# Involution on one core: the kernel products of two units issued together, their accumulations behind both

## The chip, the core and the metric

The program runs on one core of a Trainium2 chip. The metric is device time in microseconds (us) of one execution, and the median over the runs is compared.

## The reference, cut to what matters

A pair representation z of 64 x 64 positions and 32 channels goes through two triangle multiplications, two triangle attentions and a transition (not touched here), and then through an involution of 5 x 5 taps whose kernel is computed from the pixel itself:

```
z = relu(gamma * (x @ w1 + b1 - mean) / sqrt(var + 1e-3) + beta)     # 32 -> 8 channels
kern = (z @ w2 + b2).reshape(B, H, W, 25, 8)                          # 25 taps x 8 groups
patches = 25 shifted images of the padded x                           # (.., 25, 4, 8)
out = einsum('bhwpg,bhwpng->bhwng', kern, patches)                    # sum over the taps
```

## The kernel before

An image lies as 128 partitions by 1024 columns: four blocks of 16 rows, each with 32 channels on its own 32 partitions. One PSUM bank holds 512 columns, so every tile is computed in two halves (`ch` 0 and 1).

The involution is cut into 25 units (`UNITS`). Units 0 to 4 ("B") treat the middle column of taps for all four blocks at once, with the whole 128 rows of TensorE. Units 5 to 24 ("A") are `i` = 0 to 4 times `g` = 0 to 3: unit 5 + 4i + g treats block g and, stacked on the four groups of 32 partitions, the four horizontal shifts of tap row i. Its kernel product contracts 32 partitions only, those of block g (row group g of TensorE). So two units next to each other always use different row groups.

A unit passes through these steps, each on its own engine with its own queue in program order:

- TensorE computes the kernel product, two matmuls (halves) into two banks of one of three kernel buffers, `kern_banks(u)` = buffer u % 3 (L1544 for B, L1546 for A), and raises `inv_kern` with the second.
- For a unit in `ON_DVE`, VectorE adds the bias and multiplies by the shifted image in one instruction, PSUM to a product buffer (L1102). For one in `ON_POOL` = (1, 5, 8, 10, 13, 16, 20, 22), ScalarE evicts the kernel to `gate` or `th` (L832) and GpSimd multiplies (L590).
- TensorE adds the products up in banks 0 and 1 by matmuls with the identity (`ident`, accumulations n = 0 to 3, one B unit each, L1524) or with a stacked identity (`stackid`, n = 4 to 8, four A units each in four column groups, L1526). An fp32 matmul shows as two MATMUL instructions in the profile. Accumulation (n, ch) waits for the products of its units.

TensorE's order is written out by hand: units in turn, and behind each what the table `ACC_AFTER` lists for it:

```
ACC_AFTER = {5: ((1, 0), (1, 1)), 6: ((2, 0),), 7: ((3, 0),), 9: ((0, 0),), 11: ((0, 1),), 14: ((2, 1), (4, 0)),
             17: ((3, 1), (4, 1)), 19: ((5, 0),), 20: ((5, 1),), 23: ((6, 0), (6, 1)), 24: ((7, 0), (7, 1), (8, 0), (8, 1))}
```

Before its kernel product, unit u waits until unit u - 3 has left the kernel buffer: until VectorE's product (`inv_prod_dve`) or ScalarE's eviction (`inv_kbuf`) of it. There are 16 product buffers; units 16 to 24 wait for the accumulation of the unit whose buffer they take (`inv_acc`). Units 3, 4 and 5 have an extra dummy matmul ahead of them (`keep_warm`, L1116). The images that the A units read are copied into place by DMAs from SyncE (L469). When the last accumulation is done, VectorE and ScalarE copy the two result halves and they are stored.

Of the kernel before, what the change touches and what calls it, by code (L numbers as in the profile page):

```python
# [25 lines left out]
C = 32  # L26
# [8 lines left out]
KS = 5  # L35
# [26 lines left out]
def build_program(nc, z_rows, z_cols, vecs, consts, selrow, tm_w, tm_rows, ta_w, ta_qk, pt_w, inv_w1, inv_w2, out):  # L62
    with ExitStack() as ctx:
        def sb(name, cols, dt=F32, parts=128):
            return ctx.enter_context(nc.sbuf_tensor(name, [parts, cols], dt))
# [10 lines left out]
        def shared(name):  # L76

            for norm in NORMS:
                if name in (norm + "_xn", norm + "_x"):
                    return "ln_" + name[len(norm) + 1:], 2 * [n for n in NORMS if n not in LN_BIAS_FOLDED].index(norm)  # L80
                if name.startswith(norm + "_"):
                    return "ln_" + name[len(norm) + 1:], 2 * NORMS.index(norm)
            if name == "tm1_gtanh":
                return name, 0
            if name[:4] == "tail" and name[5] == "_":
                return "tail" + name[5:], 3 * int(name[4])
            for kind in ("tm", "ta"):
                if name[:2] == kind and name[2] in "01" and name[3] == "_":
                    return kind + name[3:], int(name[2]) * RAISES.get(name[4:], 2)
            return name, 0  # L90

        def sig(name):

            name = shared(name)[0]
            if name not in signals:
                signals[name] = ctx.enter_context(nc.semaphore(name))
            return signals[name]
# [22 lines left out]
        def K(name):  # L120
            i = CONST.index(name)
            return cst[:, 128 * i:128 * i + 128]
# [14 lines left out]
        w2s = sb("w2s", 2 * KS * 128, F32R)  # L137
# [61 lines left out]
        zst = sb("zst", F, F32R)  # L199
# [10 lines left out]
        def half(buf, ch):  # L210
            return buf[:, ch * HALF:(ch + 1) * HALF]
# [92 lines left out]
        def cols_of(buf, m):  # L304
# [7 lines left out]
        UNITS = [("B", i, None) for i in range(KS)] + [("A", i, g) for i in range(KS) for g in range(GB)]  # L312
# [5 lines left out]
        ACC_AFTER = {5: ((1, 0), (1, 1)), 6: ((2, 0),), 7: ((3, 0),), 9: ((0, 0),), 11: ((0, 1),), 14: ((2, 1), (4, 0)),  # L318
                     17: ((3, 1), (4, 1)), 19: ((5, 0),), 20: ((5, 1),), 23: ((6, 0), (6, 1)), 24: ((7, 0), (7, 1), (8, 0), (8, 1))}
# [42 lines left out]
        def kern_banks(i):  # L362
            return psum[:, (2 + 2 * (i % 3)) * HALF:(4 + 2 * (i % 3)) * HALF]
# [7 lines left out]
        WARM_UNITS = (3, 4, 5)  # L371
# [737 lines left out]
        def _(pe):  # L1109
            mm = nc.tensor.matmul  # L1110

            def keep_warm(b, n, operand=cst):


                for _ in range(n):
                    mm(bank[b][:, 0:256], operand[:, 0:128], operand[:, 0:256], start=True, stop=True, skip_group_check=True)  # L1116
# [391 lines left out]
            def wait_product(u):  # L1508

                if u == 0:  # L1510
                    pe.wait_ge(sig("inv_sum"), 1)
                elif u in ON_POOL:
                    pe.wait_ge(sig("inv_prod_pool"), ON_POOL.index(u) + 1)
                else:
                    pe.wait_ge(sig("inv_prod_dve"), ON_DVE.index(u) + 1)

            def accumulate(n, ch):

                for u in ACCUMULATE[n]:
                    wait_product(u)  # L1520
                for u in ACCUMULATE[n]:
                    kind, i, g = UNITS[u]
                    if kind == "B":
                        last = mm(bank[ch], K("ident"), half(prod[u % NPROD], ch), start=n == 1, stop=False, skip_group_check=True)  # L1524
                    else:
                        last = mm(bank[ch][C * g:C * g + C, :], stackid[:, :], half(prod[u % NPROD], ch), start=False, stop=n == 8,  # L1526
                                  skip_group_check=True)
                if n == len(ACCUMULATE) - 1:
                    last.then_inc(sig("inv_done"), 1)
                elif ch == 1:  # L1530
                    last.then_inc(sig("inv_acc"), 1)

            for u, (kind, i, g) in enumerate(UNITS):
                if u in WARM_UNITS:
                    keep_warm(0, 1)
                if u >= 3:
                    if u - 3 in ON_POOL:
                        pe.wait_ge(sig("inv_kbuf"), ON_POOL.index(u - 3) + 1)
                    else:
                        pe.wait_ge(sig("inv_prod_dve"), ON_DVE.index(u - 3) + 1)  # L1540
                for ch in range(2):
                    pe.wait_ge(sig("inv_zst"), ch + 1)
                    if kind == "B":
                        last = mm(half(kern_banks(u), ch), w2s[:, (KS + i) * 128:(KS + i + 1) * 128], half(zst, ch), start=True, stop=True)  # L1544
                    else:
                        last = mm(half(kern_banks(u), ch), w2s[C * g:C * g + C, i * 128:(i + 1) * 128], half(zst, ch)[C * g:C * g + C, :],  # L1546
                                  start=True, stop=True)
                last.then_inc(sig("inv_kern"), 1)
                for n, ch in ACC_AFTER.get(u, ()):
                    accumulate(n, ch)  # L1550


# [104 lines left out]
```

## Time and profile before

| | us |
|---|---|
| median of 3 runs | 228.76 (228.7 to 229.5) |
| profiled execution | 229.4 |
| its span in the profile | 226.9 |
| TensorE busy | 207.0 |
| VectorE busy | 140.9 |
| ScalarE busy | 126.7 |
| GpSimd busy | 96.0 |

Times in the rows count from the start of the span. Busy time of an engine leaves out its waits and its register work. The ends of matmuls are modelled, and matmuls overlap, so the distance between two starts says more than the length of one. A row of the timeline merges instructions of one kind that follow each other and gives their number; the time in brackets is the idle time before them and the instruction that ended it.

### The profile page before, as it was taken

Reading aid. Unit: us, or ns where it says so; the run is one execution under the profiler, and the core shown is the slowest. Engines: PE = TensorE matmul, PEld = TensorE weight load, DVE = VectorE, ACT = ScalarE, POOL = GpSimd, SP = SyncE. Lnnn points to the kernel's source line nnn. Section 1 sums busy time; section 2 is a strip of 40 time slices with the busy share of each in tenths; the row PEclk is TensorE's granted clock in tenths of the full one; section 3 lists DMA queues with packets and bytes.
Section 4 is the critical chain, followed back from the end, with each engine's and each line's share of the span. In section 5 each row is a group of like instructions: output and inputs, shape, how many; then the busy total and the mean of one; then the engine's idle time right before and its main releaser. Section 6 shows DMA issues by size and latency. Waiting matters only on the chain.

```text
span 226.9 us, 6554 instructions
## 1 busy us (share of the span) xinstructions
PE 207.0 (91%) x2758; PEld 110.2 (49%) x2758; DVE 140.9 (62%) x257; ACT 126.7 (56%) x220; POOL 96.0 (42%) x111
## 2 busy tenths in 40 slices
PE   7999989899888999999996999998999977899994
PEld 4476724675243535555663454455565413533330
DVE  0353735534694775778766275596787565857772
ACT  2758795573574759555573566874458462215131
POOL 7000004840131333975760004379458236477670
PEclk9999999999999999999999999999999999999999
DMA  6606600415024100000000010000000016400002
GB/s 202 234 7 156 249 0 6 148 43 181 4 91 106 23 3 3 0 3 4 3 3 4 12 27 0 0 3 3 3 3 3 3 49 195 130 21 0 0 3 92
DMA packets 6907, 11.45 MB, mean 50 GB/s; under 512 B 2176, under 2 KB 4096, under 8 KB 6720
## 3 DMA queue, kind: packets, MB, share of 16 engines
q1 hardware_dynamic: 6112, 10.34, 14.6%
q10 hardware_dynamic: 576, 0.70, 0.9%
q8 instruction: 22, 0.36, 0.6%
q14 instruction: 5, 0.04, 0.1%
q0 software_dynamic: 192, 0.00, 0.1%
HBM read 8.26 MB, written 2.79 MB: 49 GB/s over the span
## 4 chain that ended last, share of the span: by engine, by line
PE 71%; DVE 10%; ACT 7%; POOL 5%; issue 3%; DMA 2%; ACTq 0%; DVEq 0%; POOLq 0%
PE psum L1375 7%; PE psum L1318 7%; PE psum L1351 6%; PE psum L1526 4%; PE psum L1345 4%; PE psum L1446 4%; PE psum L1546 4%; PE psum L1524 4%; PE psum L1216 3%; PE psum L1124 3%; PE psum L1197 3%; PE psum L1135 3%; PE psum L1361 2%; PE psum L1422 2%; DMA gate<-tm_rows 2%
## 5 line engine op out<-in xcount | busy, mean ns | idle before, releaser
L548 POOL TENSOR_TENSOR soft<-soft,rinv 128x512 f32<-128x512 f32 x32 | 33.2, 1046 | 28.2 <-DVE rinv L1033 27.8
L759 ACT ACTIVATE soft<-psum 128x512 f32<-128x512 f32 x32 | 19.1, 597 | 22.9 <-PE psum L1375 22.9
L1024 DVE TENSOR_REDUCE mx<-psum 128x8 fp32r<-128x512 f32 x32 | 21.5, 681 | 14.5 <-PE psum L1351 14.5
L1030 DVE TENSOR_REDUCE rsum<-soft 128x8 f32<-128x512 f32 x32 | 21.4, 670 | 1.0 <-ACT soft L753 1.0
L1375 PE MATMUL psum<-cst,soft 128*128 128x128 f32 x128 | 20.6, 283 | 1.6 <-POOL soft L548 1.1
L1375 PEld LDWEIGHTS psum<-cst,soft 128*128 128x128 f32 x128 | 14.0, 141 | 12.8 <-issue 7.2
L753 ACT ACTIVATE soft<-psum 128x512 f32<-128x512 f32 x32 | 18.6, 595 | 1.0 <-PE psum L1361 1.0
L539 POOL TENSOR_SCALAR gth<-gth 128x512 f32<-128x512 f32 x16 | 9.7, 637 | 22.2 <-ACT gth L746 22.2
L1351 PE MATMUL psum<-Y,x 32*64 32x256 f32 x256 | 17.5, 387 | 0.0
L491 POOL COPY abv<-z1T 128x1024 f32<-128x1024 f32 x1 | 1.9, 1946 | 32.0 <-DVE z1T L958 32.0
L1318 PE MATMUL psum<-x,wyh 128*128 128x512 f32 x32 | 15.3, 612 | 0.0
L1446 PE MATMUL psum<-soft,abv 64*32 64x64 f32 x1024 | 14.7, 222 | 0.7 <-ACT soft L759 0.6
L1361 PE MATMUL psum<-mx,identr 128*128 128x512 f32 x32 | 14.5, 473 | 0.0
L1446 PEld LDWEIGHTS psum<-soft,abv 64*32 64x32 f32 x1024 | 9.5, 106 | 7.6 <-issue 6.6
L1052 DVE TENSOR_TENSOR og<-gth,psum 128x256 f32<-128x256 f32 x20 | 9.8, 492 | 4.5 <-PE psum L1446 4.4
L1345 PE MATMUL psum<-bst,pairr 128*128 128x512 f32 x32 | 12.2, 461 | 0.0
L1351 PEld LDWEIGHTS psum<-Y,x 32*64 32x64 f32 x256 | 8.2, 131 | 7.9 <-issue 5.8
L1005 DVE COPY Y<-psum 128x512 f32<-128x512 f32 x8 | 5.5, 691 | 10.2 <-PE psum L1318 10.2
L603 ACT ACTIVATE lnroom<-psum 128x512 f32<-128x512 f32 x10 | 6.0, 596 | 10.0 <-PE psum L1124 10.0
L746 ACT ACTIVATE gth<-psum,halfgb 128x512 f32<-128x512 f32 x16 | 9.7, 689 | 2.4 <-PE psum L1339 2.4
L1124 PE MATMUL psum<-og,cst 128*128 128x512 f32 x16 | 8.4, 625 | 2.5 <-DVE og L954 2.3
L1135 PE MATMUL psum<-lnroom,cst 128*128 128x512 f32 x20 | 10.0, 621 | 0.0
(197 smaller groups left out, 435.6 us busy)
## 6 DMA issues: line engine op xcount, KB each, us to landing
gth<-inv_w SPq DMA_DIRECT2D x1, 1600.0 KB, 9.7
hop<-abv SPq DMA_DIRECT2D x2, 512.0 KB, 2.9
abv<-hop SPq DMA_DIRECT2D x8, 128.0 KB, 2.9
abv<-xhop SPq DMA_DIRECT2D x4, 204.0 KB, 3.4
tmw<-tm_w SPq DMA_DIRECT2D x2, 384.0 KB, 4.4
abv<-xhop SPq DMA_DIRECT2D x4, 136.0 KB, 3.2
z0R<-z_rows SPq DMA_DIRECT2D x2, 256.0 KB, 3.5
z0T<-z_cols SPq DMA_DIRECT2D x1, 512.0 KB, 6.4
```

The costliest lines, as they stand in the source:

```text
L548: pool.tensor_tensor(PN[u % 2][:, :].rearrange("p (a k) -> p a k", k=N), E_[u % NE][:, :].rearrange("p (a k) -> p a k", k=N), rinv[:, 8 * ...
L753: nc.scalar.activation(E_[t % NE], bank[t % 4], ACT.Exp).then_inc(sig(f"{st}_exp"), 1)
L759: nc.scalar.activation(PT[u % 2], t_bank(u), ACT.Copy).then_inc(sig(f"{st}_PT"), 1)
L1024: nc.vector.tensor_reduce(mx[:, 8 * t:8 * t + 8], bank[t % 4].rearrange("p (a k) -> p a k", k=N), AX_X, ALU.max, negate=True).then_inc(sig ...
L1030: nc.vector.tensor_reduce(rsum[:, 8 * u:8 * u + 8], E_[u % NE].rearrange("p (a k) -> p a k", k=N), AX_X, ALU.add).then_inc(sig(f"{st}_sum" ...
L1135: mm(bank[vb[ch]], K("mean"), half(sq[sset], ch), start=True, stop=True, skip_group_check=True).then_inc(sig(f"{name}_var"), 1)
L1318: mm(bank[YBANKS[ch][h]], wyh[:, s * 512 + h * 128:s * 512 + (h + 1) * 128], half(x, ch), start=True, stop=True).then_inc(sig(f"{st}_yproj ...
L1345: mm(bank[t % 4], pairr[:, :], bst[:, :], start=True, stop=False, skip_group_check=True)
L1351: last = mm(bank[t % 4][64 * i2:64 * i2 + 64, :].rearrange("p (h a k) -> p h a k", h=H, a=2)[:, :, a, :], x[C * g:C * g + C, r * N:(r + 1) ...
L1361: mm(bank[t % 4].rearrange("p (a k) -> p a k", k=N), identr[:, :], mx[:, 8 * t:8 * t + 8].unsqueeze(2).broadcast_to([128, 8, N]), start=Fa ...
L1375: last = nc.tensor.transpose(t_bank(u)[:, 128 * h:128 * h + 128], PN[u % 2][:, 128 * h:128 * h + 128], K("ident"))
L1446: last = mm(bank[av_banks(u)[a]][C * h:C * h + C, 64 * i2:64 * i2 + 64], vals[64 * a:64 * a + 64, v0 + C * h:v0 + C * h + C], PT[u % 2][64 ...
```

## The change

Units 0 to 4 are issued one by one as before. From unit 5 on they are issued in pairs (5, 6), (7, 8), to (23, 24). For a pair, TensorE first waits for the kernel buffers of both units, then issues half 0 of the first, half 0 of the second, half 1 of the first, half 1 of the second, and then the accumulations that the table lists for either. The table, the buffers and the other engines' programs stay as they are.

```diff
-            for u, (kind, i, g) in enumerate(UNITS):
-                if u in WARM_UNITS:
-                    keep_warm(0, 1)
+            def kernel_buffer_free(u):
                 if u >= 3:
                     if u - 3 in ON_POOL:
                         pe.wait_ge(sig("inv_kbuf"), ON_POOL.index(u - 3) + 1)
                     else:
                         pe.wait_ge(sig("inv_prod_dve"), ON_DVE.index(u - 3) + 1)
+            def unit_kernel(u, ch):
+                kind, i, g = UNITS[u]
+                pe.wait_ge(sig("inv_zst"), ch + 1)
+                if kind == "B":
+                    last = mm(half(kern_banks(u), ch), w2s[:, (KS + i) * 128:(KS + i + 1) * 128], half(zst, ch), start=True, stop=True)
+                else:
+                    last = mm(half(kern_banks(u), ch), w2s[C * g:C * g + C, i * 128:(i + 1) * 128], half(zst, ch)[C * g:C * g + C, :],
+                              start=True, stop=True)
+                if ch == 1:
+                    last.then_inc(sig("inv_kern"), 1)
+
+            for together in [(u,) for u in range(KS)] + [(u, u + 1) for u in range(KS, len(UNITS), 2)]:
+                for u in together:
+                    if u in WARM_UNITS:
+                        keep_warm(0, 1)
+                    kernel_buffer_free(u)
                 for ch in range(2):
-                    pe.wait_ge(sig("inv_zst"), ch + 1)
-                    if kind == "B":
-                        last = mm(half(kern_banks(u), ch), w2s[:, (KS + i) * 128:(KS + i + 1) * 128], half(zst, ch), start=True, stop=True)
-                    else:
-                        last = mm(half(kern_banks(u), ch), w2s[C * g:C * g + C, i * 128:(i + 1) * 128], half(zst, ch)[C * g:C * g + C, :],
-                                  start=True, stop=True)
-                last.then_inc(sig("inv_kern"), 1)
-                for n, ch in ACC_AFTER.get(u, ()):
-                    accumulate(n, ch)
+                    for u in together:
+                        unit_kernel(u, ch)
+                for u in together:
+                    for n, ch in ACC_AFTER.get(u, ()):
+                        accumulate(n, ch)
```

## Rows read from the trace of the kernel before

**Rows 1.** The page: busy time by engine, and TensorE's granted clock in 40 slices.

```profile
PE 207.0 (91%) x2758; PEld 110.2 (49%) x2758; DVE 140.9 (62%) x257; ACT 126.7 (56%) x220; POOL 96.0 (42%) x111
...
PEclk9999999999999999999999999999999999999999
```

**Rows 2.** Stretch: busy PE, PEld, DVE, ACT, POOL; granted clock, DMA share, GB/s.

```profile
197.50:223.80 26.30, 26.24 (x137) 8.63 (x136) 18.64 (x16) 7.81 (x8) 18.20 (x9) 1.00 0.06 17
```

**Rows 3.** Chain of waits, 197.6 to 223.8: shares, then start, length, what.

```profile
by line: PE psum L1526 36.1%; PE psum L1546 32.1%; PE psum L1524 31.5%; ACT Y L834 2.3%; PE psum L1116 0.8%; issue 0.1%
...
197.66 0.67 PE psum L1546 x2
198.32 1.91 PE psum L1524 x4
200.23 0.65 PE psum L1546 x2
200.88 1.06 PE psum L1524 x2
...
203.65 0.67 PE psum L1546 x4
...
205.37 0.87 PE psum L1546 x4
...
216.69 0.94 PE psum L1546 x5
217.63 1.85 PE psum L1526 x16
...
220.15 3.62 PE psum L1526 x32
```

**Rows 4.** Timeline of TensorE in the stage: start, length, line, operation, count.

```profile
200.16 0.72 PE L1546 MATMUL psum<-zst,w2s 32*128 32x512 f32 x2
...
203.58 0.74 PE L1546 MATMUL psum<-zst,w2s 32*128 32x512 f32 x4
...
207.23 1.21 PE L1546 MATMUL psum<-zst,w2s 32*128 32x512 f32 x6
...
213.32 0.73 PE L1546 MATMUL psum<-zst,w2s 32*128 32x512 f32 x4
213.98 0.63 PE L1526 MATMUL psum<-og,stackid 128*32 128x512 f32 x3
...
223.15 0.59 PE L1526 MATMUL psum<-og,stackid 128*32 128x512 f32 x1
```

**Rows 5.** Timeline of VectorE: products of units 3, 6, 9, 11, 18 and 19, 24.

```profile
196.66 1.27 DVE L1102 SCALAR_TENSOR_TENSOR gth<-psum,vec,soft 128x1024 f32<-128x1024 f32 x1
...
201.02 1.28 DVE L1102 SCALAR_TENSOR_TENSOR lnroom<-psum,b2shift,abv 128x1024 f32<-128x1024 f32 x1 [1.90 <-PE psum L1546]
...
204.49 1.28 DVE L1102 SCALAR_TENSOR_TENSOR og<-psum,b2shift,abv 128x1024 f32<-128x1024 f32 x1 [0.47 <-PE psum L1546]
206.38 1.28 DVE L1102 SCALAR_TENSOR_TENSOR og<-psum,b2shift,abv 128x1024 f32<-128x1024 f32 x1 [0.61 <-PE psum L1546]
...
214.29 2.47 DVE L1102 SCALAR_TENSOR_TENSOR gth<-psum,b2shift,abv 128x1024 f32<-128x1024 f32 x2 [0.53 <-PE psum L1546]
...
220.38 1.28 DVE L1102 SCALAR_TENSOR_TENSOR og<-psum,b2shift,abv 128x1024 f32<-128x1024 f32 x1 [0.32 <-PE psum L1546]
```

**Rows 6.** Timeline of ScalarE: eviction of unit 8.

```profile
204.35 1.11 ACT L832 ACTIVATE gate<-psum,b2shift 128x1024 f32<-128x1024 f32 x1 [4.88 <-PE psum L1546]
```

**Rows 7.** Timeline of GpSimd: products of units 5 and 22.

```profile
200.58 2.36 POOL L590 TENSOR_TENSOR lnroom<-th,abv 128x1024 f32<-128x1024 f32 x1
...
219.28 2.38 POOL L590 TENSOR_TENSOR lnroom<-th,abv 128x1024 f32<-128x1024 f32 x1
```

**Rows 8.** The shifted images' transfers, by tile: length, first and last start.

```profile
L469 SPq DMA_DIRECT2D abv<-xhop x12: 303/424/429, 187.3 to 196.6; - x12
```

**Rows 9.** Timeline of TensorE around its longest pause in this execution.

```profile
68.89 1.05 PE L1312 MATMUL psum<-x,taw 128*32 128x512 f32 x4 [1.15 <-DVE x L848]
```

## The prediction

> **What bounds the kernel now.** The page comes first: TensorE is busy for 207.0 of 226.9 us, and the granted clock is full in every slice [rows 1]. That is an average, so I read only the stage that the diff touches, the involution from unit 5 on. In the window from 197.5 to 223.8 TensorE is busy for 26.24 of 26.30 us, VectorE for 18.64, GpSimd for 18.20 and ScalarE for 7.81 [rows 2]. The chain of waits says the same in order of time: from 197.66 to 223.77 it is TensorE alone, kernel products (L1546) and accumulations (L1524, L1526) in turn, then ScalarE's last copy and the store [rows 3]. By the chain's shares of that window (26.2 us) the kernel products take 32.1%, which is 8.41 us.
>
> The reader should see two things in it. First, what a group of kernel products costs. Unit 5 alone holds the chain for 0.67 us, unit 6 for 0.65; units 8 and 9, issued one behind the other, hold it for 0.67 together [rows 3]. The 32-row products of two row groups thus already run side by side. Where the group costs more (10 and 11: 0.87; 21 to 23: 0.94), a unit in it waited for its PSUM buffer. Second, TensorE has no pause, though there are only three kernel buffers: unit u waits until unit u-3 has been multiplied or evicted. Behind each kernel product stand accumulations of 0.86 to 2 us, and they are the cover under which the buffers come free.
>
> **The round trip of a buffer.** Kernel products of one or two units end 0.72 to 0.74 us behind their start, and the next block on TensorE can begin after 0.65 to 0.67 [rows 3, 4]. VectorE starts a product 0.14 behind that end (201.02 after 200.16 + 0.72; 0.17 at unit 9: 204.49 after 204.32), and 0.24 behind it from unit 17 on (214.29 after 213.32 + 0.73; 0.23 at unit 24); it takes 1.28 [rows 4, 5]. TensorE goes on 0.05 behind that: unit 11's product ends at 207.66, and unit 14, which waits for it, must have begun at 208.44 - 0.72 = 207.72 [rows 4, 5]. The round trip is 0.73 + 0.14 + 1.28 + 0.05 = 2.20 us, 2.29 from unit 17 on. For a unit evicted by ScalarE (start 0.04 behind the product, 1.11 long) it is 0.73 + 0.04 + 1.11 + 0.05 = 1.93 [rows 4, 6].
>
> **The change part by part.** No instruction of arithmetic is added, and no DMA is touched. The order by halves inside a pair costs and gains nothing: units 8 and 9 were issued as two halves, then two halves, and their four products took 0.74 us all the same [rows 4]. What works is the grouping. A pair u, u+1 now waits for u-3 and for u-2 before its first product, and u-2 is the first unit of the pair before. So whenever that unit is VectorE's, two pairs that follow each other can't start closer than 2.20 (2.29) us, however little TensorE has between them. I lay the ten pairs out with these steps: 0.66 for a pair, as for units 8 and 9; then accumulations, whose instructions step 0.43 (the last 32, four at a time, took 3.62 = 8 x 0.43 + 0.18). One half with the identity is 1.05 (1.06 for unit 6's), two are 1.91, three would be 1.91 + 2 x 0.43 = 2.77. Two stacked halves are 1.85, one is 1.85 - 2 x 0.43, about 1.00 [rows 3].
>
> 5,6: wait for unit 3's product, 196.66 + 1.27 + 0.05 = 197.98, where before the products began at 197.66 + 0.67 - 0.74 = 197.59: pause 0.40. Three accumulations follow, to 201.41.
> 7,8: 201.41, no wait. VectorE multiplies unit 7 from 202.28 to 203.56. Its unit 6 needs the shifted image, and GpSimd, which reads the same image, began at 200.58 [rows 7]; so 6 ends by 201.9 and holds nothing up.
> 9,10: TensorE is ready at 203.12, unit 7 frees the buffer at 203.61: pause 0.49.
> 11,12: 203.61 + 2.20 = 205.81, ready at 205.32: 0.49.
> 13,14: 208.01, ready at 207.52: 0.49.
> 15,16: TensorE has two accumulations and is ready at 210.72; the buffers are free (unit 12 at 209.2, unit 13, ScalarE's, at 209.9).
> 17,18: nothing is accumulated behind 15,16, since no entry of the table has key 15 or 16. Ready at 211.38, but unit 15's product comes at 212.92: pause 1.54.
> 19,20: two accumulations cover the round trip (215.21): starts at 215.63.
> 21,22: likewise (217.92): 218.14.
> 23,24: again nothing behind 21,22. Ready at 218.80; unit 21 is free at 218.14 + 2.29 = 220.43: pause 1.63.
> Then six halves without a change of mode: from 221.09, 48 matmuls that step 0.43 per four, so 221.09 + 12 x 0.43 + 0.19 = 226.44, against 223.74 (223.15 + 0.59) before [rows 4]. The inputs of the last of them are there: VectorE ends unit 24 at 223.9 and GpSimd (2.38 each) unit 22 at 222.5, and accumulation 8 begins at 224.5 [rows 5, 7].
>
> The same as a sum. Kernel products: 8.41 - 10 x 0.66 = 1.81 saved. Changes between accumulation blocks that now touch: 0.20 + 0.15 + 0.14 = 0.49 saved (1.91 + 1.06 becomes 2.77; 1.00 + 1.00 becomes 1.85; 1.85 + 3.62 = 5.47 becomes 5.35, about 0.13). Pauses: 0.40 + 3 x 0.49 + 1.54 + 1.63 = 5.04 lost. Together +2.7 us. ScalarE's copy and the store behind it move along. The profiled execution took 229.4 us (span 226.9 and 2.5 around it), so it becomes 232.1; the median of the runs is 228.76, 0.6 lower, and becomes 231.5.
>
> Bounds of the parts. The signal from product to VectorE is read at 0.14 to 0.17 early and 0.23 to 0.24 late: I take 0.14, and 0.03 more in three pauses is +0.1. Whether all ten pairs run as close as 8 and 9 did isn't shown; 0.66 is the nearest row (also 18 and 19), and the far end is the 0.87 of units 10 and 11, which would give up to 10 x 0.21 = +2.1 if nothing waited; I take 0.66, because 0.87 contains a wait. GpSimd's 2.0 to 2.4 us per product decide nothing, with about 2 us to spare at unit 22. The shifted image lands after the last of its 12 transfers, issued by 196.6 [rows 8]; it would have to be over 0.5 us later than here to matter, and 1 us later would add 0.4. Below, the pauses can't vanish without a shorter round trip; if it were 0.2 shorter at each of the five pauses that hang on it, the sum would be +1.7.
>
> A page speaks for this change and against it. The Trainium skill, TensorEngine Tiling (Array Packing), Theoretical Speedup, gives up to four times the rate where the contracted side is 32 or less; taken alone, that is rival A below. The same page, Performance Considerations, warns that tiling speeds TensorE and not the emptying of PSUM; by that, the 2.20 us round trip sets the pace, as the schedule says. The rows bear out the first for units 8 and 9, and the second in units 11, 14, 22 and 23, which waited in the kernel before.
>
> **The rivals.** The bound for telling a change from none is 0.5%, 1.14 us here.
>
> A, faster: the buffers are free when TensorE arrives, and only the savings stand: 1.81 + 0.49 = 2.3 us, 228.76 - 2.3 = 226.5. For it: TensorE is the whole chain, and its groups get cheaper. Against it: it needs the first product of each pair back within what TensorE has between two pairs, and that is 0.66 us in two places and 1.71 in three, against 2.20. It turns at pauses of 2.3 us in sum; the two places without an accumulation alone make 3.2. 5%.
>
> B, no change that can be told: the pauses are there but smaller, say only those two and half of the rest: 3.2 + 0.9 - 2.3 = +1.8 is still slower, so it needs them at 0.5 to 0.6 of their size as well: round trips near 1.6 us, sum about +0.8, 229.6. No row has a round trip that short: VectorE's own 1.28 stands in it. 7%.
>
> C, much slower by the clock: the two long pauses are longer than any that TensorE has now. The longest, 1.15 us before 68.89, left the granted clock at 1.00 [rows 1, 9]. If it fell to its lower level after 220.4, the 6.0 us behind it would double at most, giving up to 237.5. Against it: 1.15 and 1.54 are close, and TensorE is dense on both sides. 4%.
>
> D, the change doesn't do what it says: the products of a pair don't run side by side. Then a pair costs two single blocks, 1.31 instead of 0.66, and ends later, so the round trip grows as well: 10 x 0.65 = +6.5 on top, 238. Units 8 and 9 speak against it [rows 4]. 2%.
>
> **How the numbers follow.** The forecast as laid out has 82%. Slower by over 0.5% holds the forecast, C and D: 0.88. Within 0.5%: B, 0.07. Faster: A, 0.05. The predicted time is that of the forecast, 231.5. The range: below, the shorter round trip (+1.7) less 0.2 for the spread of the runs, 230.2; above, the late signal, a late image and some of the bound for pairs (+0.1, +0.4, +0.3) and the 0.6 by which single executions lie above the median, 232.9. It leaves out A, B, C, D and little more.
>
> **What the profile after would show.** Right: the first product of pair 17,18 about 1.5 us behind the last of 15,16's end, the same before 23,24, both put down to VectorE; pauses near 0.5 before 9, 11 and 13; TensorE's busy time in the stage down and its end at about 226.4; four products of a pair within 0.74 us; VectorE idle before the first unit of each pair. Wrong: no pause before 17,18 (round trip misread), pairs that take 0.9 or more (D), a granted clock under 1 after 212 (C), or the time lost elsewhere than in the pauses, say in GpSimd's products.

## The result: 2% slower, and the profile after

The changed kernel takes 234.03 us (median of 4 runs, 233.34 to 235.39) against 229.13 for the kernel before, a ratio of 1.0204 with a 95% interval of 1.0153 to 1.0256. That is +4.9 us where +2.7 was forecast, and outside the range that I gave. Repeated later, beside other runs of the kernel before, it was 1.0195 (1.0156 to 1.0234). Medians are over all runs, while the ratios leave out runs more than 1.5% above the fastest of the same kernel, so a ratio can differ a little from the quotient of two medians. The profiled execution took 233.54 us (span 231.0, that of before 226.9).

The chain of waits of the kernel after, from unit 3's product on (start, length, what):

```profile
197.44 0.09 issue
197.53 0.73 PE psum L1548 x4
198.26 2.77 PE psum L1524 x6
201.03 0.70 PE psum L1548 x4
...
203.21 0.75 PE psum L1548 x4
...
207.23 0.43 issue
207.66 0.73 PE psum L1548 x4
...
210.44 0.70 PE psum L1548 x4
...
211.23 1.30 DVE z2R L1102
...
212.62 0.73 PE psum L1548 x4
213.35 1.63 PE psum L1524 x2
214.97 1.87 PE psum L1526 x8
216.84 0.80 PE psum L1548 x4
217.64 1.85 PE psum L1526 x16
219.50 0.71 PE psum L1548 x4
220.21 0.03 issue
220.23 1.12 ACT th L832
221.35 0.42 issue
221.78 0.73 PE psum L1548 x4
222.51 5.33 PE psum L1526 x48
```

What was TensorE alone [rows 3] is now broken by VectorE and by waits. Ten pairs (L1548, x4) stand in it, each at 0.70 to 0.80 us. The reader should then look at the two pieces behind 212.62. One half of an identity accumulation takes 1.63 where it took 1.06 [rows 3], and eight stacked matmuls take 1.87 where the schedule had 1.00. Nothing waits inside them. The next view says why. It is busy time by stretch of the kernel after: PE, PEld, DVE, ACT, POOL, then the granted clock, DMA share and GB/s.

```profile
197.10:213.70 16.60, 13.39 (x52) 4.92 (x52) 10.47 (x10) 5.57 (x5) 12.73 (x7) 1.00 0.09 24
213.70:217.10 3.40, 3.40 (x12) 0.54 (x12) 2.33 (x2) 0.00 (x0) 0.66 (x1) 0.50 0.00 0
217.10:227.80 10.70, 9.09 (x76) 2.61 (x74) 5.74 (x5) 2.23 (x2) 4.75 (x2) 1.00 0.01 2
```

From 213.7 to 217.1 the granted clock is 0.50, so the array runs at 1.2 instead of 2.4 GHz; in the same stage of the kernel before it was 1.00 throughout [rows 2]. The fall comes behind TensorE's first long pause. Its timeline in the kernel after (the brackets give the pause and who ended it):

```profile
197.53 0.73 PE L1548 MATMUL psum<-zst,w2s 32*128 32x512 f32 x4 [0.38 <-DVE gth L1102]
...
203.21 0.73 PE L1548 MATMUL psum<-zst,w2s 32*128 32x512 f32 x4 [0.46 <-DVE lnroom L1102]
...
205.44 0.74 PE L1548 MATMUL psum<-zst,w2s 32*128 32x512 f32 x4 [0.44 <-ACT th L832]
...
207.66 0.73 PE L1548 MATMUL psum<-zst,w2s 32*128 32x512 f32 x4 [0.43 <-issue]
...
210.37 0.74 PE L1548 MATMUL psum<-zst,w2s 32*128 32x512 f32 x4
212.62 0.73 PE L1548 MATMUL psum<-zst,w2s 32*128 32x512 f32 x4 [1.51 <-DVE z2R L1102]
...
219.43 0.74 PE L1548 MATMUL psum<-zst,w2s 32*128 32x512 f32 x4
221.78 0.73 PE L1548 MATMUL psum<-zst,w2s 32*128 32x512 f32 x4 [1.61 <-ACT th L832]
...
227.21 0.59 PE L1526 MATMUL psum<-og,stackid 128*32 128x512 f32 x1
```

The pauses stand before 5,6, before 9,10, 11,12, 13,14, before 17,18 and before 23,24, the six places of the forecast and no other. The last is put down to ScalarE; its eviction of unit 22 began at 220.23 and has nothing to do with the buffers of 23 and 24. VectorE's product of unit 21, from 220.39 to 221.67, ended 0.1 us before the pair began. Nor is it ScalarE before 11,12: its eviction of unit 8 ended at 205.10, VectorE's product of unit 9 at 205.33, again 0.1 us before the pair. In VectorE's timeline of the kernel after, its wait for the kernel product stands before the first unit of the pair:

```profile
211.23 1.28 DVE L1102 SCALAR_TENSOR_TENSOR z2R<-psum,b2shift,abv 128x1024 f32<-128x1024 f32 x1 [1.29 <-PE psum L1548]
...
220.39 1.28 DVE L1102 SCALAR_TENSOR_TENSOR lnroom<-psum,b2shift,abv 128x1024 f32<-128x1024 f32 x1 [1.24 <-PE psum L1548]
```

To compare kernels without what lies ahead of the change, I measure the stage from the end of the last middle-column product (unit 4) to the end of the last accumulation. The kernel before, in its timeline of TensorE, ends unit 4 here:

```profile
196.41 0.81 PE L1544 MATMUL psum<-zst,w2s 128*128 128x512 f32 x2
```

So its stage is 223.74 - 197.22 = 26.5 us, with the end from [rows 4]. In the kernel after, unit 4 ends at 196.72 and the stage at 227.21 + 0.59 = 227.80: 31.1 us, +4.6.

### The profile page after: what moved, and what is told of

Same layout as the page of the kernel before. It is cut to its first block, busy times and chain, and to the rows that moved or that the text cites. A ratio compares the mean times of both kernels' runs of the same rounds, so it can differ in the third digit from the quotient of the medians.

```text
span 231.0 us, 6544 instructions
## 1 busy us (share of the span) xinstructions
PE 206.4 (89%) x2758; PEld 109.5 (47%) x2758; DVE 141.0 (61%) x257; ACT 126.7 (55%) x220; POOL 96.0 (42%) x111
## 4 chain that ended last, share of the span: by engine, by line
PE 70%; DVE 12%; ACT 8%; issue 4%; POOL 3%; DMA 1%; ACTq 0%; DVEq 0%; POOLq 0%
PE psum L1375 7%; PE psum L1318 6%; PE psum L1351 6%; PE psum L1526 4%; PE psum L1124 4%; PE psum L1345 4%; PE psum L1446 4%; PE psum L1135 4%; PE psum L1216 3%; PE psum L1548 3%; PE psum L1197 3%; PE psum L1524 3%; PE psum L1361 2%; PE psum L1422 2%; PE psum L1339 2%
## 5 line engine op out<-in xcount | busy, mean ns | idle before, releaser
L548 POOL TENSOR_TENSOR soft<-soft,rinv 128x512 f32<-128x512 f32 x32 | 33.2, 1044 | 28.2 <-DVE rinv L1033 27.7
L1548 PE MATMUL psum<-zst,w2s 32*128 32x512 f32 x40 | 7.5, 446 | 4.8 <-ACT th L832 2.0
```

The source lines that it names most:

```text
L548: pool.tensor_tensor(PN[u % 2][:, :].rearrange("p (a k) -> p a k", k=N), E_[u % NE][:, :].rearrange("p (a k) -> p a k", k=N), rinv[:, 8 * ...
```

## The experiments

Nine more kernels were run, and the change once more. The three medians of the kernel before belong to e1 to e4, e5 to e8, and e9 and e10; the change's first ratio is to the 229.13 above. "Full clock" counts the runs whose granted clock was at least 0.998 over the span. The stage is that of one profiled execution of each kernel; the change and its repetition differ by 0.07 us in it.

| kernel | median us | ratio to before (95%) | runs at full clock | stage us |
|---|---|---|---|---|
| before | 230.1, 229.9, 229.91 | | 24 of 57 | 26.5 |
| the change | 234.03 | 1.0204 (1.0153 to 1.0256) | 0 of 4 | 31.1 |
| the change again (e5) | 233.98 | 1.0195 (1.0156 to 1.0234) | 0 of 6 | 31.1 |
| dummies in both pauses (e1) | 233.12 | 1.0100 (1.0055 to 1.0146) | 3 of 6 | 29.4 |
| waits apart (e2) | 235.5 | 1.0217 (1.0164 to 1.0269) | 0 of 6 | 30.3 |
| half by half alone (e3) | 230.21 | 1.0003 (0.9972 to 1.0034) | 6 of 12 | 26.8 |
| accumulations in the pauses (e4) | 232.42 | 1.0053 (1.0018 to 1.0087) | 5 of 12 | 28.2 |
| dummies in the first pause (e6) | 234.88 | 1.0209 (1.0158 to 1.0259) | 0 of 6 | 31.1 |
| one joint wait (e7) | 233.5 | 1.0174 (1.0130 to 1.0218) | 0 of 6 | 30.2 |
| accumulations by threes (e8) | 228.18 | 0.9953 (0.9921 to 0.9986) | 7 of 12 | 25.3 |
| table refined (e9) | 227.59 | 0.9901 (0.9866 to 0.9935) | 8 of 12 | 24.9 |
| one dummy in each pause (e10) | 234.57 | 1.0187 (1.0144 to 1.0230) | 0 of 6 | 31.0 |

More than half of the runs of the kernel before (33 of 57) have a mean clock under 0.998 too. Where their lower stretch stands isn't shown, since its one profile is at full clock. But in the profiles of e2, e4, e6 and e10 such stretches stand some 75 or some 130 us ahead of the stage, where the program is that of before. In e2, e4 and e10 one of them begins inside the 1.15 us pause of [rows 9]. This is the pause in e10, with the stretch behind it by engine (the granted clock is the third number from the end):

```profile
68.59 1.92 PE L1312 MATMUL psum<-x,taw 128*32 128x512 f32 x4 [1.15 <-DVE x L848]
...
69.00:71.80 2.80, 2.80 (x6) 0.84 (x3) 0.64 (x2) 0.59 (x1) 0.00 (x0) 0.50 0.63 187
```

The same pause in the same program left the clock at 1.00 in the other nine profiles. Such stretches come and go from run to run with every kernel, so the profiled stage is the cleaner measure of what a schedule costs; the ratios, over a mixture of both, say whether it can be told from nothing.

**e1: dummies in both long pauses.** The first wait is for a free buffer, so the dummies can write it before the second wait ends.

```diff
                     kernel_buffer_free(u)
+                    if u in (17, 23):
+                        keep_warm(2 + 2 * (u % 3), 3)
```

> The changed kernel with three dummy matmuls (about 0.43 us each, 1.3 in all) between the wait for unit 17's buffer and that for unit 18's, and again between those of 23 and 24, so in the two pauses of 1.5 and 1.6 us; they write the free kernel buffer. Theory: the joint waits cost 2.7 us and the rest of the measured +4.9 is the granted clock, which fell because TensorE paused there. Then the clock stays at 1.000 in every run, the starts of pairs 17,18 and 23,24 stay about 1.5 and 1.6 us behind, and the time is 2.5 to 3.0 us over the kernel before (about 231.8). Rival: the clock falls for another reason (a chance of the chip, or the sparser work of the whole stage); then the clock stays at 0.985 to 0.992 and the time at +4.3 to +5.5. Second rival: the dummies themselves delay the pairs; then +3 or more at a full clock.

Measured: three of six runs at full clock, and not all six as I had expected; of the 23 runs of the kernel before that were taken beside it, 9 were. The median of the three is 231.94 against 229.49 for those nine, +2.45; the ratio is 1.0100. The stage is 29.4, 2.9 over before and 1.7 under the change. In the timeline of TensorE the dummies fill the pause and the pair starts 2.2 us behind the one before it, as without them:

```profile
210.66 0.74 PE L1548 MATMUL psum<-zst,w2s 32*128 32x512 f32 x4
211.33 1.56 PE L1116 MATMUL psum<-cst 128*128 128x256 f32 x6
212.87 0.74 PE L1548 MATMUL psum<-zst,w2s 32*128 32x512 f32 x4
```

So the schedule costs 2.9 us of the stage and the clock 1.7. The change had no run at full clock in ten, this kernel three in six, and only the idleness of TensorE was changed: the rival that the clock in the stage fell for another reason falls. So does the one that the dummies delay the pairs.

**e2: each unit waits for itself.** The accumulations stay behind both.

```diff
-                    kernel_buffer_free(u)
-                for ch in range(2):
-                    for u in together:
-                        unit_kernel(u, ch)
+                    kernel_buffer_free(u)
+                    for ch in range(2):
+                        unit_kernel(u, ch)
```

> Accumulations behind both units as in the change, but each unit waits for its own buffer alone and both its halves are issued at once, as before. Theory (the round trip of a buffer rules): laid out by the prediction's steps, the first units of pairs start earlier, but the second ones, and so all accumulations behind, still wait for the first unit of the pair before: +2.2 us at a full clock (231.3), with the two long waits now before units 18 and 24 and TensorE's pauses there cut to about 1 us. If the clock falls all the same, +3.8 to +5. Rival: the joint wait is the whole loss, and placing the accumulations behind both costs nothing; then the kernel is within 0.5 us of the kernel before.

Measured: 1.0217, no run at full clock, stage 30.3, +3.8. A stretch at the lower clock lies in it: in its chain of waits, eight stacked matmuls take 1.62 us instead of 1.00 and sixteen 2.29 instead of 1.85. That is about 1.1 us, and leaves 2.7 for the schedule, against 2.9 with the joint wait (e1) and 2.2 given. Its timeline of TensorE around units 17 and 18:

```profile
214.78 0.74 PE L1548 MATMUL psum<-zst,w2s 32*128 32x512 f32 x6
216.98 0.73 PE L1548 MATMUL psum<-zst,w2s 32*128 32x512 f32 x2 [1.46 <-DVE z2R L1102]
```

Unit 17 slips in beside 15 and 16 (x6), and unit 18 waits alone. I had expected TensorE's pause to shrink to 1 us; it stayed at 1.46, because unit 17 ran beside the others and not behind them. The +3.8 is what I had given for a fallen clock. The rival, that the joint wait is the whole loss, falls: what costs is that all accumulations stand behind the second unit, and the joint wait adds some 0.2 us by this estimate.

**e3: half by half alone.**

```diff
-            for together in [(u,) for u in range(KS)] + [(u, u + 1) for u in range(KS, len(UNITS), 2)]:
+            for together in [(u,) for u in range(KS)] + [(5,), (6,), (7,), (8, 9), (10, 11), (12, 13), (14,), (15, 16), (17,), (18, 19), (20,), (21, 22), (23,), (24,)]:
```

> Only units between which the kernel before has no accumulation go together half by half (8,9; 10,11; 12,13; 15,16; 18,19; 21,22), so every accumulation keeps its place. Theory: the order by halves is worth nothing and the joint waits that are left cost 0.2 us each in two places and run beside others: +0.2 us by the steps (229.3), clock 1.000. Rival: issuing halves in turn costs by itself (weights reloaded between row groups, later signals), about 0.1 to 0.2 us a pair: then +0.8 us or more, and a pair's four products take over 0.8 us.

Measured: 1.0003 (0.9972 to 1.0034), stage 26.8, +0.3. In the timeline of TensorE units 8 and 9 take what they took before [rows 4], in the other order of halves:

```profile
203.45 0.73 PE L1548 MATMUL psum<-zst,w2s 32*128 32x512 f32 x4
```

The order by halves is worth nothing and costs nothing that can be told; the +0.3 of the stage is of the size of the joint waits left in it, pauses of 0.19, 0.16 and 0.15 us before 10,11, before 12,13 and before 21,22.

**e4: accumulations moved into the pauses.** The change with its table altered in three places.

```diff
-14: ((2, 1), (4, 0)),
-17: ((3, 1), (4, 1)), 19: ((5, 0),), 20: ((5, 1),), 23: ((6, 0), (6, 1)), 24: (...)
+14: ((2, 1),), 16: ((4, 0),),
+17: ((3, 1), (4, 1)), 19: ((5, 0),), 22: ((5, 1), (6, 0)), 23: ((6, 1),), 24: (...)
```

> The changed kernel with its table altered: the first half of accumulation 4 moves from behind 13,14 to behind 15,16, the second half of 5 and the first of 6 to behind 21,22. Nothing else. Theory: the two long pauses shrink to about 0.55 before 17,18 and nothing before 23,24, a pause of 0.65 opens before 21,22; by the steps +1.4 us, and the clock stays full since no pause is above 0.7: about 230.5. Rival: it is the pairs and not the empty places that cost; then it stays above +2.5.

Measured: stage 28.2, +1.7 (given: +1.4), granted clock 1.00 all through it (the lower stretches of this execution, 234.86 us in all, stand ahead of it), ratio 1.0053. The five runs at full clock have a median of 230.55 us, +1.1 over the nine of before beside them; that it is the 230.5 I gave is luck, since that number stood on a lower median of before. Three quarters of the loss of the ratio are gone with pairs, halves and joint waits all in place, so it is where the accumulations stand and not the pairs as such.

**e5: the change again.** No edit.

> The change itself once more, beside the other kernels of this call. Theory: every run holds one stretch at the lower clock behind the pause before 17,18, as all four did so far (clock 0.985 or 0.992, never 1.000); the ratio stays near 1.02, about +4.6 us over runs of the kernel before. Rival: the low stretch was a chance of four runs; then some runs show 1.000 and stay at +2.7.

Measured: 233.98, 1.0195, no run above 0.993. Where the lower stretch stands is seen in the profiled execution alone; the other runs have only a mean clock. The low stretch in its profile begins 16.7 us behind the end of unit 4, in that of the first 17.0, both within 1.1 us of the end of the pause before 17,18.

**e6: dummies in the first pause only.** Shown against e1.

```diff
-                    if u in (17, 23):
+                    if u == 17:
```

> The changed kernel with the three dummy matmuls in the first long pause (before pair 17,18) alone; the pause of 1.6 us before 23,24 stays. Theory: it was the first pause, with the pauses of 0.45 us ahead of it, that brought the clock down; if the second one alone doesn't, the time is that with both sets of dummies, +2.7 to +3.0 us, and runs at 1.000 occur. Rival: any pause of this length does it; then no run is at 1.000, a low stretch stands behind 23,24, and the time is about +4.4.

Measured: 1.0209, no run at full clock, stage 31.1 again. My theory that the second pause is harmless falls, and the rival stands. Busy time by stretch in this kernel (the granted clock is the third number from the end): full until behind the second pause, then low.

```profile
214.00:223.60 9.60, 7.99 (x52) 2.97 (x55) 6.29 (x5) 3.25 (x3) 5.77 (x4) 1.00 0.00 0
...
224.60:227.80 3.20, 3.20 (x20) 0.79 (x16) 1.69 (x2) 0.00 (x0) 0.29 (x1) 0.51 0.00 0
```

The 48 matmuls of the end take 7.03 us here and 5.33 in the change, 1.7 more. In the change the same second pause was not followed by a fall in either profile, which show one each, behind the first pause. So each long pause can bring it, and filling only the first did not rid the kernel of it.

**e7: one joint wait.** Only 17 and 18 go as a pair.

```diff
-[(u, u + 1) for u in range(KS, len(UNITS), 2)]:
+[(u,) for u in range(KS, 17)] + [(17, 18)] + [(u,) for u in range(19, len(UNITS))]:
```

> The order of the kernel before, but units 17 and 18 go as a pair (joint wait, halves in turn, accumulations behind both); one long pause and no others. Theory: laid out by the prediction's steps this costs +2.0 us at a full clock (the pause of 1.5 us and more waits before 23). If that pause alone brings the clock down, +3.5 and no run at 1.000; if it takes the sparser work of the pairs ahead of it too, runs at 1.000 occur and the time is +2.0. Rival: the loss of the change lies in the pairs altogether; then this one costs a tenth of it, 0.5 us.

Measured: 1.0174, no run at full clock, stage 30.2, +3.7; +3.5 was given for a fallen clock. In its chain of waits all is as before up to 15,16, and then:

```profile
210.89 0.72 PE psum L1548 x4
...
211.69 1.29 DVE z2R L1102
...
213.08 0.73 PE psum L1548 x4
213.81 1.60 PE psum L1524 x2
215.41 1.87 PE psum L1526 x8
217.27 0.83 PE psum L1548 x2
```

One pause of 1.5 us, with no others ahead of it in the stage, carries four fifths of the change's loss. By the chain, 1.60 + 1.87 + 0.83 us behind it, against 1.06 + 1.00 + 0.66 at full clock, put about 1.6 of the 3.7 down to the clock; the 2.1 left is the wait, 2.0 given. This is the smallest edit that shows both.

**e8: accumulations by threes.** The kernel before, and only the table is changed: as many units go one behind another as there are buffers, each waiting for itself.

```diff
+        ACC_AFTER = {5: ((1, 0), (1, 1)), 8: ((2, 0), (3, 0)), 11: ((0, 0), (0, 1)), 14: ((2, 1), (3, 1)), 17: ((4, 0), (4, 1)),
+                     20: ((5, 0), (5, 1)), 23: ((6, 0), (6, 1)), 24: ((7, 0), (7, 1), (8, 0), (8, 1))}
```

> The kernel before with another table and nothing else: units in threes, as many as there are kernel buffers, each waiting for itself; accumulations stand behind 5, 8, 11, 14, 17, 20, 23, 24, two halves together each. Theory: the gain that the change was after (fewer, fuller groups of kernel products, fewer changes between accumulations) is there if no unit waits for a product of its own group: by the steps -1.4 us against the kernel before (about 0.6% faster), with waits of 0.8 to 0.9 inside three groups. Rival: whatever is pushed together pays in waits as the change did; then no gain or slower.

Measured: 0.9953 (0.9921 to 0.9986), stage 25.3, -1.2 where -1.4 was given. The seven runs at full clock have a median of 227.57, 1.0 under the seven such runs of before beside them (228.59).

**e9: the table refined.**

```diff
+        ACC_AFTER = {5: ((1, 0),), 8: ((1, 1), (3, 0), (0, 0)), 11: ((0, 1),), 12: ((3, 1),), 15: ((5, 0),), 17: ((2, 0), (2, 1)),
+                     20: ((4, 0), (6, 0), (4, 1)), 23: ((5, 1), (7, 0)), 24: ((7, 1), (6, 1), (8, 0), (8, 1))}
```

> The kernel before with a table that is no longer plain threes: (1,0) behind 5; (1,1), (3,0), (0,0) behind 8; (0,1) behind 11; (3,1) behind 12; (5,0) behind 15; (2,0), (2,1) behind 17; (4,0), (6,0), (4,1) behind 20; (5,1), (7,0) behind 23; the rest behind 24. By the steps of the prediction -1.6 us against the kernel before, where the table by threes had -1.4 and its stage measured -1.24 (25.27 us from the end of unit 4's kernel product to the last accumulation, against 26.51). Theory: stage at 25.1, ratio near 0.994, full clock. Rival: the steps are not fine enough for 0.3 us; then it is no better than the table by threes or worse.

Measured: 0.9901 (0.9866 to 0.9935), 227.59 us, stage 24.9, -1.6 as given. It beats both kernels. The ratio is a little better than 1.6 us would make it (0.993, inside the interval); part of that is that more of its runs were at full clock, 8 of 12 against 8 of 17. Runs at full clock alone give 227.35 against 229.30, -1.9. Its stage in busy time by stretch shows TensorE as full as before, in a shorter time:

```profile
197.50:222.20 24.70, 24.39 (x137) 8.26 (x136) 18.34 (x16) 7.82 (x8) 18.18 (x9) 1.00 0.06 16
```

**e10: one dummy in each long pause.** Shown against e1.

```diff
-                        keep_warm(2 + 2 * (u % 3), 3)
+                        keep_warm(2 + 2 * (u % 3), 1)
```

> The changed kernel with one dummy matmul (two instructions, 0.43 us) in each long pause instead of three, so TensorE's pauses are about 1.1 us there instead of 1.5 and 1.6. The schedule is the same, so a full clock gives +2.8 and a low stretch +4.5. If the length of the single pause decides, as the 1.15 us pause that left the clock full in the kernel before suggests, then runs at 1.000 occur and the time is +2.8. Rival: any further sparseness behind the pauses of 0.45 us is enough; then no run at 1.000.

Measured: 1.0187, no run at full clock, stage 31.0: the rival stands. The timeline of TensorE has only 0.84 us of pause left, and the accumulation behind it still takes 1.78:

```profile
212.78 0.70 PE L1116 MATMUL psum<-cst 128*128 128x256 f32 x2
214.32 0.73 PE L1548 MATMUL psum<-zst,w2s 32*128 32x512 f32 x4 [0.84 <-DVE z2R L1102]
214.99 1.78 PE L1524 MATMUL psum<-lnroom,cst 128*128 128x512 f32 x2
```

No run of six at full clock with pauses of 0.84 and 0.94 us in the stage, while the pause of 1.15 us elsewhere left the clock alone in nine of twelve profiles [rows 9]. The length of the single pause is thus no sufficient reading; what else counts, the runs don't settle.

## Why the prediction was wrong

**The round trip of a buffer: right.** Pairs 9,10 to 13,14 start at 203.21, 205.44 and 207.66, 2.23 and 2.22 us apart; 2.20 was given. Pair 17,18 follows 15,16 by 2.25 and 23,24 follows 21,22 by 2.35, given 2.20 and 2.29. The Trainium skill (TensorEngine Tiling (Array Packing), Performance Considerations) warns that tiling doesn't speed the emptying of PSUM; here VectorE's 1.28 us are the largest part of the 2.2, while a pair's products hold TensorE for 0.66, so the trace agrees.

**The cost of a pair: right.** Four products within 0.73 to 0.74 us at full clock; the order by halves worth nothing (e3).

**The pauses and the sum of the schedule: right in place, a little short in size.** 2.7 was given; the stage with a full clock (e1) is 2.9 longer. The round trips are 0.02 to 0.06 longer each, which carries on from pair to pair. The savings are there: 2.77 for three accumulation halves, 5.33 for 48 stacked matmuls. Two small slips in the working change nothing: the last blocks that touch save 0.12 by their own figures (5.47 - 5.35), not 0.14, and the shortest accumulations behind a kernel product hold the chain for 0.99 us, not 0.86.

**The clock: the step that failed.** The sum has no term for the granted clock. Under rival C I gave its fall a 4% chance, since a pause of 1.15 us left it at 1.00 and "1.15 and 1.54 are close". It fell in both profiles of the change, and none of its ten runs was at full clock. It costs 1.7 us in the stage (31.1 against 29.4 with the pauses filled), where I had priced up to 6.0, and it comes behind the first long pause, not after 220.4. By rows: 1.63 + 1.87 + 0.80 us after against 1.05 + 1.00 + 0.66 is 1.6. Added to the forecast of 2.7 the 1.6 gives 4.3, near the 4.6 of the stage. The chance was the mistake: one pause that did no harm in one execution was taken for a bound. In three of the twelve profiles the clock is at 0.50 right behind that very pause, so the row held less than I read from it, and it stands 130 us ahead of the stage. With 1.6 for the clock the forecast would have been 233.1. Of the 0.9 left up to 234.03, 0.2 is the round trips and 0.4 the median of the kernel before, which was 229.13 beside the change and 228.76 when I forecast; 0.3 stays open.

**Rivals A, B and D.** A and B needed round trips under what TensorE has between two pairs; none was. D needed pairs of 0.9 us or more at full clock; none is.

**What the change was worth in itself.** Fewer groups of kernel products and fewer changes between accumulations do save time, as e8 and e9 show. The change paid for them: each pair waits for the first unit of the pair just before it, and in two places TensorE has no accumulation to do in the meantime.

## What to carry to other kernels

When work is grouped to fill an engine better, write down for every group what it waits for and what the engine has to do in the meantime; a group with nothing between it and the next pays the whole round trip of its buffer. Group as many units as there are buffers, let each wait for itself, and spread the covering work evenly: here a table alone then gained 0.7% by the stage (1.0% by the ratio) where the pairs lost 2%. And treat any new pause of TensorE of about a microsecond in a dense stage as a risk to its clock, priced beside the wait; here dummies that write a free buffer bought that part back, 1.7 us. A pause that left the clock full in one execution is no bound; look at the same pause in several.

## What the runs showed of the hardware

Four kernels with one or two pauses of 0.84 to 1.61 us left in this stage (e2, e6, e7, e10) and the change itself had no run at full clock in 34; with the pauses filled or at most 0.61 us (e1, e4) 8 of 18 were, about as many as of the kernel before (24 of 57). In each of the six profiles of the former (the change has two) the clock is lower once in the stage, from 0.8 to 2.0 us after the end of a long pause on (212.62 to 213.7 in the change). While it lasts, the step of four stacked matmuls is 0.86 us instead of 0.43.

The pause alone doesn't tell. With two long pauses in the stage, one of them is followed by no fall in any profile. The 1.15 us pause of [rows 9], in the same program each time, left the clock at 1.00 in nine profiles and in three (e2, e4, e10) a stretch at 0.50 begins inside it, 0.05 to 0.65 us before its end. And pauses of 0.93 and 1.01 us shortly ahead of the stage left it at 1.00 in all twelve. What decides, of the work around a pause and of chance from run to run, is open.
